# First attention layer: the keys' last third moved to the next batch's first pair, its stash to the second; at a group's end the last query first and the output projection in eighths

## What is computed

```python
q_hk = (hidden_q @ Wq.T).reshape(Bv, Sv, H, K)          # H = 16 heads
q_big = jnp.einsum('bshk,hkq->bshq', q_hk, w_kc_q)
q_big = _apply_rope(q_big, sin_q[None, :, None, :], cos_q[None, :, None, :])
kv_r = _apply_rope(kv_c, sin_k[None], cos_k[None])      # 32 x 1500 x 64
q_r = jnp.einsum('bshq,hqr->bhsr', q_big, W_qr)
k_r = jnp.einsum('bld,hdr->bhlr', kv_r, W_kr)
scores = jnp.einsum('bhsr,bhlr->bhsl', q_r, k_r)
attn = jax.nn.softmax(scores, axis=-1)
ctx_c = jnp.einsum('bhsl,bld->bhsd', attn, kv_r)
ctx_lat = jnp.einsum('bhsd,hkd->bhsk', ctx_c, w_kc_kv)
return ctx @ Wo.T
```

## Time and profile before

| | |
|---|---|
| median of three runs | 2970.72 us (2968.65 to 2975.44) |
| the profiled execution | 2962.2 us, span 2960.4 us |
| PE busy | 2721.3 us (92%) |
| DVE / ACT / POOL busy | 1926.2 / 1129.2 / 1791.0 us |
| DMA | 209.21 MB, mean 71 GB/s |
| granted TensorE clock, mean | 0.96 |

### The profile page before, as it was taken

How to read it: one execution, slowest core, us unless ns; L and a number is a source line. 1 busy time by engine, 2 the same in 40 slices (tenths; PEclk the granted TensorE clock), 3 DMA queues, 4 the chain that set the end, 5 groups by cost and what they waited for, 6 DMA issues and landing times. The chain is left out here.

```text
span 2960.4 us, 43403 instructions
## 1 busy us (share of the span) xinstructions
PE 2721.3 (92%) x16024; PEld 1696.8 (57%) x16024; DVE 1926.2 (65%) x2382; ACT 1129.2 (38%) x1641; POOL 1791.0 (60%) x1175
## 2 busy tenths in 40 slices
PE   7689999999999999996799979999999999997998
PEld 6445554555555555553688855555555555555665
DVE  3487776776677586745766656765765765665674
ACT  2124441444144513442433324443443443442331
POOL 0369985997689866992300029787877877950111
PEclk9689999999999999997999989999999999998998
DMA  9333340344123321422000043323232332301000
GB/s 301 107 82 95 89 114 26 78 100 115 40 70 90 100 72 43 100 58 107 1 1 1 1 93 89 80 68 84 65 88 69 80 82 66 88 7 50 7 7 13
DMA packets 98842, 209.21 MB, mean 71 GB/s; under 512 B 30306, under 2 KB 74322, under 8 KB 91116
## 3 DMA queue, kind: packets, MB, share of 16 engines
q1 hardware_dynamic: 98636, 206.44, 27.3%
HBM read 135.36 MB, written 46.00 MB: 61 GB/s over the span
## 5 line engine op out<-in xcount | busy, mean ns | idle before, releaser
L1432 DVE TENSOR_REDUCE maxpart<-pair 112x2 f32<-112x1000 f32 x748 | 896.3, 1198 | 416.2 <-PE pair L1058 411.9
L1245 ACT ACTIVATE prob<-wide 125x896 f32<-125x896 f32 x768 | 672.8, 918 | 779.6 <-PE wide L1084 566.4
L1312 POOL TENSOR_TENSOR sums<-sums,prob 125x448 f32<-125x448 f32 x544 | 689.5, 1288 | 53.7 <-POOL sums L1312 45.1
L1315 POOL TENSOR_TENSOR sums<-sums,prob 125x896 f32<-125x896 f32 x284 | 615.1, 2166 | 116.6 <-ACT prob L1245 79.2
L1098 PE MATMUL single<-prob,kv 125*64 125x448 f32 x3072 | 672.0, 551 | 0.7 <-ACT prob L1245 0.7
L1079 PE MATMUL wide<-qhigh,kparts 64*125 64x448 f32 x3072 | 445.7, 367 | 0.3 <-DVE maxpart L1432 0.3
L1058 PE MATMUL pair<-kparts,qhigh 64*112 64x500 f32 x1496 | 337.1, 446 | 51.3 <-DVE maxpart L1432 41.0
L1098 PEld LDWEIGHTS single<-prob,kv 125*64 125x64 f32 x3072 | 211.5, 136 | 253.4 <-issue 189.8
L1058 PEld LDWEIGHTS pair<-kparts,qhigh 64*112 64x112 f32 x1496 | 131.0, 172 | 351.7 <-DVE maxpart L1432 177.2
L1079 PEld LDWEIGHTS wide<-qhigh,kparts 64*125 64x125 f32 x3072 | 283.7, 183 | 57.6 <-issue 29.2
L1084 PE MATMUL wide<-shift,ones_row 64*125 64x448 f32 x1536 | 283.5, 364 | 0.2 <-DMA shift<-maxrow 0.2
(11 more groups left out here) (407 smaller groups left out, 4017.9 us busy)
## 6 DMA issues: line engine op xcount, KB each, us to landing
kparts<-keys_merged SPq DMA_DIRECT2D x64, 750.0 KB, 8.9
kparts<-kparts SPq DMA_DIRECT2D x96, 250.0 KB, 3.1
keys_merged<-kparts SPq DMA_DIRECT2D x32, 750.0 KB, 10.4
recip<-zrec_merged SPq DMA_DIRECT2D x124, 112.0 KB, 2.8
w_low_values<-w_merged SPq DMA_DIRECT2D x64, 192.0 KB, 2.8
raw<-in_ctx SPq DMA_DIRECT2D x32, 375.0 KB
values_merged<-kv SPq DMA_DIRECT2D x32, 375.0 KB
kv<-values_merged SPq DMA_DIRECT2D x32, 375.0 KB
```

What stands on the lines that cost most here:

```text
L1245: nc.scalar.activation(prob[:, n_ % NPROB, :].rearrange("p (a b) -> p a b", a=2), acc[0:LP, :, 0:HQ], ACT.Exp)\
L1312: nc.gpsimd.tensor_tensor(dst[:, cols], first_in[:, cols], prob[:, n_ % NPROB, cols], ALU.add)\
L1315: nc.gpsimd.tensor_tensor(dst, first_in, prob[:, n_ % NPROB, :], ALU.add).then_inc(s["pool_sum"], 1)
L1432: V.tensor_reduce(maxpart[:, b % 2, t:NMAX:4, third], acc[0:TQ, :, 0:LB], AX.X, ALU.max).then_inc(*R.signal_drained(kind, *key))
```

## The change

It changes the list of steps of the first layer only, in two places.

Inside a group, for all batches but a group's first, the last third of batch b+1's keys now stands in pair 0 of batch b (it stood in pair 5 of batch b-1), and its stash in pair 1 behind `norm` (it stood in pair 5 of batch b-1). In a group's last batch the third of batch b+2 stays in pair 4 and its stash in pair 5. `raw` is ordered with the second third (pair 3). `ropecos` part 1 goes from pair 0 to pair 5 before it, and `mean` of the next group ahead of pair 5's `mix`. 

At a group's end the last query comes after two of the next batch's maxima instead of three, the projection is cut into eight pieces instead of four, and these stand between the maxima; `maxT` comes before the last two maxima. `Regions` and all semaphores' meanings stay; the projection's waits are moved to the new piece numbers.

```diff
@@ attention_schedule, end of a group @@
-            for i in range(3):
-                maximum(first + 1, i, (0, PAIR, 0)[i])
-            if g:
-                add("attn", g - 1, 0, region=1)
+            def output(*pieces):
+                for piece in pieces:
+                    if g:
+                        add("attn", g - 1, piece, region=None if piece else 1)
+
+            maximum(first + 1, 0, 0)
+            maximum(first + 1, 1)
             add("query", g, NPAIR - 1, region=2)
-            for c in range(3):
-                add("smax", first, 3, c, region=(PAIR, 0, PAIR)[c])
-            if g:
-                add("attn", g - 1, 1)
-                add("attn", g - 1, 2)
+            output(0)
+            add("smax", first, 3, 0, region=PAIR)
+            add("smax", first, 3, 1, region=0)
+            output(1)
+            add("smax", first, 3, 2, region=PAIR)
+            output(2)
             add("maxneg", first)
+            add("maxT", first, region=3)
+            output(3)
+            maximum(first + 1, 2, 0)
+            output(4, 5)
             maximum(first + 1, 3)
-            add("maxT", first, region=3)
-            if g:
-                add("attn", g - 1, 3)
+            output(6, 7)
@@ the pairs of a batch @@
-                if p == 5 and j < BG - 1 and b + 2 < NB:
-                    add("keyT", b + 2, 2, region=3)
+                if p == 0 and j and b + 1 < NB:
+                    add("keyT", b + 1, 2, region=3)
+                if g + 1 < G and j == BG - 2 and p == 5:
+                    add("mean", g + 1, region=3)
                 if j or p:
                     old = (b, t - 2) if p else (b - 1, LT - 2)
...
-                if p == 0 and 1 <= b and b + 2 < NB:
-                    add("ropecos", b + 2, 1)
+                if p == 5 and b + 3 < NB:
+                    add("ropecos", b + 3, 1)
                 if p == 4 and j == BG - 1 and b + 2 < NB:
                     add("keyT", b + 2, 2, region=3)
-                if p == 5 and b + 2 < NB:
+                if p == 1 and j and b + 1 < NB:
+                    add("stash", b + 1)
+                if p == 5 and j == BG - 1 and b + 2 < NB:
                     add("stash", b + 2)
...
-                if g + 1 < G and j == BG - 2 and p == 5:
-                    add("mean", g + 1, region=3)
@@ SyncE @@
-                if kind == "keyT" and key[1] == 2 and key[0] + 2 < NB:
+                if kind == "keyT" and key[1] == 1 and key[0] + 2 < NB:
                     b = key[0] + 2
@@ TensorE, attn @@
-                    m = piece // 2
+                    m = piece // 4
...
-                    if piece == 1 and g == G - 1:
+                    if piece == 2 and g == G - 1:
                         pe.wait_ge(s["ctx_ready"], NB + 1)
-                    for i in range(piece % 2 * H // 4, (piece % 2 + 1) * H // 4):
+                    for i in range(piece % 4 * H // 8, (piece % 4 + 1) * H // 8):
```

More of the change, by code:

```diff
@@ L201, in rolling_schedule @@
     add("tokens")
-    for piece in range(4):
+    for piece in range(8):
         add("attn", G - 1, piece, region=None if piece else 1)
@@ L1150, in _ @@
                         pe.wait_ge(s["ctx_ready"], BG * (g + 1))
-                    if piece == 1 and g == G - 1:
+                    if piece == 2 and g == G - 1:
                         pe.wait_ge(s["ctx_ready"], NB + 1)
-                    for i in range(piece % 2 * H // 4, (piece % 2 + 1) * H // 4):
+                    for i in range(piece % 4 * H // 8, (piece % 4 + 1) * H // 8):
                         mm = pe.matmul(attn_acc[:, m, 0:NT].rearrange("p (j s) -> p j s", j=BG), wvo[:, i, m * 128:(m + 1) * 128],
                                        ctx_n[:, :, i * S:(i + 1) * S], start=(i == 0), stop=(i == H // 2 - 1))
-                    if piece == 1:
+                    if piece == 3:
                         mm.then_inc(s["attn_half"], 1)
-                    if piece == 3:
+                    if piece == 7:
                         mm.then_inc(*R.signal_filled("attn", g, 0))
@@ L1524, in _ @@
                     V.tensor_tensor(x_all[:, g, m, :], region[3][:, 0:NT], x_all[:, g, m, :], ALU.add).then_inc(*R.signal_drained("project", g, m, 0))
-                elif kind == "attn" and key[1] == 3:
+                elif kind == "attn" and key[1] == 7:
                     g, _ = key
```

## The result

The changed kernel takes 3073.3 us (median of 4 runs, 3068.5 to 3079.9); the kernel before, timed beside it, 2973.1. The ratio is 1.034 (95% interval 1.0313 to 1.0367), some 100 us more. The prediction was 3034, slower. The profiled execution has a span of 3068.1 us at a mean granted clock of 0.944; before it was 2960.4 at 0.96.

The account below looks back on a forecast made before the run. GpSimd's pair additions, a 27.75 us cycle, were taken to bound the batches. Late batches and group tails 61.5, plus clock 12.7, less group ends 11, gave +63: 3034 from 2970.72. Range 2974 to 3078; the forecast case's own, 2990 to 3055.

Parts of the forecast that it names:

- (c): Stash delays the key copy before pair 4's maximum: TensorE pauses 3.15 us in 20 batches, loop 30.25 against 27.75.
- The clock in the pauses: TensorE's clock falls after half of 23 pauses, costing 1.1 us each: 12.7 us.
- (b): Pair 0: the moved third holds region 3, so `last` moves by 1.8 us; TensorE's 3.4 lead hides it, no cost.
- (d): At j = 6, `shift` ordered late behind stash and `raw`: a TensorE pause of 5.0 us, in three groups.
- Group ends: At three boundaries, query waits run under projection pieces: 3.7 us saved each, 11 together; nothing at group 0.
- no hold-up: Rival: transfers do not delay each other, copy lands 3 us after its order, only group ends count; 2960, chance 0.14.
- held less: Rival: stash lands in 8.0, copy at once; pause 1.5, loop 28.6 us; 2971 to 2987, chance 0.14.
- Every pause at the slow clock: Rival: every pause ends at the slow clock and `shift` at j = 6 comes 5 later, three times; 3062, chance 0.2.
- additions that wait for ScalarE: Sign: inside a group GpSimd's additions wait for ScalarE, not their own predecessor; no total given.
- 20 waits near 3 for `kparts<-kparts`: Sign: TensorE's maximum in pair 4 waits about 3 us for the key-third copy, 20 times.
- the late landing: Sign: the key-third copy ordered at pair 2 lands 7 to 8 us after its order instead of 3.1.
- the dips of the clock: Sign: the granted clock dips after TensorE's wait at pair 4's maximum; no size given.

Follow-up runs that it names:

- e3: Kernel before with only the stash moved to pair 1 of a group's batches 1 to 7; 3048.8 us, ratio 1.0269.
- e10: Changed kernel with only `raw` moved back to pair 5, behind `shift`; stash stays in pair 1; 3053.6 us, ratio 1.0272.
- e5: Changed kernel with stash (pair 1 in a group's last batch) and `raw` in pair 5, behind `shift`; moved third and new group ends stay; 2971.3 us.
- e12: Kernel of e11 (stash in pair 2) with the stash ordered by ScalarE instead of SyncE; 3105.2 us, ratio 1.0465.
- e4: Changed kernel with seven additional unread 128x128 matmuls ahead of pair 4's maximum in batches 1 to 5 of each group; 3039.4 us, ratio 1.0238.
- e1: Kernel before with only the new group ends (query first, projection in eighths between the maxima); 2956.1 us, ratio 0.996.
- e8: Kernel before with all moves inside the batches (third, `raw`, stash, rotation, `mean`) and the old group ends; 3085.7 us, ratio 1.0384.
- e6: Kernel before with only `raw` moved, behind the keys' second third in pair 3 instead of the last in pair 5; 2974.8 us, ratio 1.0013.
- e11: Changed kernel with the stash one pair later, in pair 2 behind the copy of third 0; 3129.9 us, ratio 1.0536.

## Why the prediction was right, and where its sizes were not

The direction, the mechanism and the place were right; the sum was +63 and came to some +100. The 3073.3 lies above the forecast's own 2990 to 3055 and above the highest rival (3062), and 5 us inside the end of the range: the width of the range carried it, not the sizes. The parts, in us, as the sum had them and as the two profiled executions show them:

| part | said | measured |
|---|---|---|
| four groups, first exponential to first `last` (the moved third's wait) | 7.2 | 7.9 |
| the batches with a pause, at full clock | 49.6 | 51.0 |
| the slow clock behind the 20 pauses | 11.0 | 32.3 |
| batch 6 of three groups, clock included | 9.7 | 15.9 |
| from the last `last` to the group's end | -3.4 | -2.1 |
| the stretches between the groups | 0 | 7.2 |
| group ends | -11 | -9.2 |
| together | 63 | 103 |

Over half of the miss is the clock. Step by step:

- **The stash holds up the copies (c): right, shown by e3 and by e10 against e5.** From `last` to the pause's end 17.6 was predicted, 17.4 to 17.7 measured at 17 of the 20; a pause of 3.15, measured 2.92 to 3.72, 20 times; a landing of 7 to 8, measured 7.5 to 8.3. e10 and e5 differ only in the place of the stash in the batches 1 to 6 of a group: 1.0272 against 1.0003, 80 us. The row of the weights at 732.27 had foretold it. I had put it down to "the queue"; by e12 the stash holds up a copy in another queue just as long, by filling the engines. The Trainium skill (DMA: Bandwidth & Descriptors, "Issuing engines are not separate DMA queues") says that all of them run on the same 16 DMA engines; e12's 8.0 and its 97.9% agree.
- **The clock in the pauses: mis-sized, the largest part of the miss.** I counted half of 23 pauses at 1.1, 12.7 us (11.0 of it for the 20). The clock fell after 17 of the 20 and all three for `shift`, and a fall cost 1.5 us or, where it took longer, 2.7: the next `last` came 12.4 after the pause's end at full clock (3 places), 13.7 to 13.95 or 15.0 to 15.2 otherwise, 14.0 on average. e4, with the same copy, puts it at 30 us. The nearer row was the wrong one to halve with: the waits of 1.50 and 1.06 cost 1.1, the longer pause costs more. The Trainium skill (TensorE: Matmul & The Clock Gate, "HAM oscillation — how this bites in real kernels") has a kernel that pays in every tile; 20 of 23 is nearer to that than my half.
- **The moved third costs nothing by itself (b): wrong, 13 us (e5 against e1).** In e5 `last` waits 2.4 in a group's first batch (1.8 predicted), and then 1.3 in every batch where nothing else is later. I set 1.8 against TensorE's lead of 3.4 at tile 2. But the wait is not for something that TensorE runs ahead of: ScalarE's copy stands behind an exponential that GpSimd releases, so the lead is gone at this very place. In the changed kernel this error did little, since the pauses make TensorE late anyway: `last` waits only in a group's first batch (4 rows, 9.7 us), and that wait was in the sum. e10 (+81) does stand 13 above what e3 and e1 give together (+80 - 12). By the two traces 5 of it are those first batches; in the twenty batches with a pause, `last` to the pause's end takes 353 us in all in both, and from there e10 takes 7 longer, because the clock fell after all twenty pauses (17 in e3). Whether the third's place makes it fall more often is not shown.
- **`shift` at batch 6 (d): right, a little short.** 5.0 predicted, 6.50, 5.59 and 5.38 measured. Half of 11.2 was a guess; e10 shows that `raw` is over half of the pause: without it 2.61, 1.96 and 1.60. Not in the sum at all was what comes behind: the stretch between the groups grew by 1.0, 3.9 and 2.3 us.
- **Group ends: right, -12 (e1) against -11.** Group 0 gave nothing, as said; the boundaries gave 2.1, 2.9 and 4.0 instead of 3.7 each.

By differences of ratios along before, e1, e5, e10, after, the change is: group ends -12, third +13, stash +80 (with its share of the clock), `raw` ahead of `zrec` +20. That they come to +101 is no evidence, since such a chain always adds up; e3 and e8 are: on the kernel before, the stash alone costs the same 80, and all moves inside the batches cost 114 (113 by the chain). `raw` alone on the kernel before costs 4 (e6); it needs the late queue to cost 20.

Of the rivals, "no hold-up" and "held less" are refuted. "Every pause at the slow clock" came nearest in time and in its clock part; its other part did not come: `shift` at batch 6 was to be 5 later still, and the pauses there were 5.4 to 6.5. What I looked for in the profile after was there: additions that wait for ScalarE (211.9 us against 112.6), 20 waits near 3 for `kparts<-kparts`, the late landing, the dips of the clock. The loop in a group's middle was said to be 30.2 and is 29.9 where the clock stays up, 31.4 to 32.8 at nearly all others.

Open: why the engines, while the stash fills them, give the other queue's copy no turn; why the clock stayed up after three of twenty like pauses (after none in e10); and whether the third can stand anywhere in pairs 0 to 4 for nothing.

## What to carry to other kernels

When a large store is moved in a queue, write down what is ordered behind it and when each is needed: here 1.1 MB that nobody waits for cost 80 us by starting 1.3 us ahead of a 250 KB copy that TensorE does wait for, and another queue did not shorten the way of a copy ordered as close behind. A lead over the bounding engine counts only against waits that don't hang on that engine: follow the wait back through each engine's queue before calling it hidden. Price a pause on a busy TensorE with what follows it, here 3 us of pause and 1.6 on average behind.

## Not expected of the hardware

- A queue of one's own gave nothing: a copy ordered 0.95 us behind 1.1 MB of another queue landed 8.0 later (e12), as in the same queue (7.7).
- An order itself gets slow when much is outstanding: the two of `packed` take 5.06 us to issue while ScalarE's stash starts (1.64 in the changed kernel), `raw` 2.39 and `zrec` 2.06 behind the stash in e11 (0.48 and 0.59 in the kernel before).
- Fourteen short matmuls, 1.83 us in a pause of three, kept the clock up at 19 of 20 places, with some 1.2 us of pause left: 30 us for work that nobody reads.
